# Column sums by GpSimd and fp32 matmuls in place of fp16 pairs, in a convolution fused with layer norms and a table-driven FFN

## What is computed

```python
def _ln_c(v): return (v - mean_c(v)) / sqrt(var_c(v) + 1e-6)       # over the 256 channels
x = x + conv3x3_mean(_ln_c(x))          # each channel by itself, all weights 1/9, zero border
t = tokens(x)                           # (8, 4096, 256)
n = (t - mean(t)) / sqrt(var(t) + 1e-5)
t = t + ffn(n)                          # ffn returns n plus the small additions below
```

## Time and profile before

| | |
|---|---|
| median of 3 runs | 748.62 us (745.1 to 753.97) |
| the profiled execution | 747.69 us, span 745.9 us |
| busy: PE, DVE, ACT, POOL | 546.9, 593.3, 496.0, 295.8 us |
| mean granted TensorE clock | 0.903 |
| DMA | 68.01 MB, mean 91 GB/s; DVE waits for a load once, 20.5 us, at the start |
| waits, in total: DVE L568 for PE | 62.6 us in 41 |
| waits, in total: PE L932 for DVE g | 67.8 us in 27 |

### The profile page before, as it was taken

The page is one execution under the profiler, slowest core; times in us unless marked ns, Lnnn a source line. Parts: engine busy times, 40 slices in busy tenths (PEclk is TensorE's granted clock), DMA queues, the critical chain, the costliest instruction groups (busy, mean ns, idle before and its releaser), DMA issues. The chain is left out here.

```text
span 745.9 us, 11144 instructions
## 1 busy us (share of the span) xinstructions
PE 546.9 (73%) x2381; PEld 268.0 (36%) x2423; DVE 593.3 (80%) x1482; ACT 496.0 (66%) x739; POOL 295.8 (40%) x580
## 2 busy tenths in 40 slices
PE   0045578888888888777889887768888888889670
PEld 0011234444434344333344343334434443444340
DVE  1679888998898888688798988968898888897240
ACT  0113677778787778747687867667788777788830
POOL 0223644544444444443244444414444444442200
PEclk9987899999999999969898989899999999999985
DMA  9999990993679544990469707940329009497999
GB/s 109 107 164 195 189 158 1 115 177 48 82 101 178 93 56 73 167 159 0 57 101 175 119 1 112 126 45 0 52 30 145 0 1 118 23 77 43 89 83 77
DMA packets 626041, 68.01 MB, mean 91 GB/s; under 512 B 625856, under 2 KB 625984, under 8 KB 625984
## 3 DMA queue, kind: packets, MB, share of 16 engines
q1 hardware_dynamic: 624496, 67.29, 79.8%
q10 hardware_dynamic: 1488, 0.17, 0.2%
HBM read 33.90 MB, written 33.55 MB: 90 GB/s over the span
## 5 line engine op out<-in xcount | busy, mean ns | idle before, releaser
L831 ACT ACTIVATE xbuf<-xbuf,shift,gain (+1 forms) x256 | 222.1, 935 | 0.0
L678 POOL TENSOR_TENSOR nlo<-n,nhi 128x1024 f16<-128x1024 f32 x64 | 152.4, 2382 | 124.0 <-ACT nhi L813 124.0
L550 DVE BATCH_NORM_STATS2 stat<-xbuf 128x6 f32 (+1 forms) x256 | 171.5, 683 | 20.6 <-DMA xbuf<-x 20.5
L910 PE MATMUL ps<-h1m,w2m 128*128 128x512 f32 x256 | 142.0, 638 | 0.0
L568 DVE TENSOR_TENSOR xbuf<-ps,xbuf 128x512 f32 (+1 forms) x128 | 90.8, 709 | 62.7 <-PE ps L871 62.6
L541 DVE TENSOR_SCALAR n<-xbuf,stat,rns 128x256 f32 (+1 forms) x256 | 133.1, 595 | 1.1
L813 ACT ACTIVATE nhi<-n 128x1024 f16<-128x1024 f32 x64 | 67.9, 1062 | 93.1 <-DVE n L541 93.1
L871 PE MATMUL ps<-nhi,band 128*128 128x512 f16 (+1 forms) x408 | 116.6, 402 | 16.1 <-POOL nlo L678 14.1
L871 PE MATMUL ps<-nlo,band 128*128 128x512 f16 (+1 forms) x408 | 119.6, 411 | 0.0
L800 ACT ACTIVATE h<-ps 128x512 f32<-128x512 f32 x128 | 76.4, 597 | 60.2 <-PE ps L913 59.7
L688 POOL TENSOR_TENSOR ut<-xbuf,stat 128x16 f32<-128x16 f32 x32 | 7.3, 227 | 252.7 <-DVE shift L469 252.7
(11 more groups left out here) (91 smaller groups left out, 651.2 us busy)
## 6 DMA issues: line engine op xcount, KB each, us to landing
xbuf<-x SPq DMA_DIRECT2D x16, 1024.0 KB, 11.6
out<-xbuf SPq DMA_DIRECT2D x32, 512.0 KB, 7.1
xbuf<-x SPq DMA_DIRECT2D x30, 512.0 KB, 7.0
out<-xbuf SPq DMA_DIRECT2D x12, 1024.0 KB, 12.8
out<-xbuf SPq DMA_DIRECT2D x16, 256.0 KB, 7.9
xbuf<-x SPq DMA_DIRECT2D x4, 256.0 KB, 8.2
consts<-cst SPq DMA_DIRECT2D x1, 170.0 KB, 2.4
h<-ws ACTq DMA_DIRECT2D x8, 10.0 KB
```

The source lines that it names most:

```text
L550: return v.bn_stats(stat[:, j % 4, at + 2 * s:at + 2 * s + 2, :].rearrange("p w n -> p (w n)"), xview(par)[:, w:w + 2, :].rearrange("p w c ...
L678: pool.tensor_tensor(nlo[:, at:at + HALF, :], n32[:, h, :, :], nhi[:, at:at + HALF, :], ALU.subtract).then_inc(lo_ready, 1)
L831: ins = act.activation(col, col, ACT.Identity, bias=shift[:, k, w:w + 1], scale=gain[:, k, w:w + 1])
L910: pe.matmul(ps[:, B_L2, :], w2m[:, :], h1m[:, i % 2, :], start=False, stop=False)
```

## The change

- n32 becomes a ring of 16 columns. POOL sums it over three neighbouring columns in fp32 into `nsum`: an edge sum of one column (it completes the last column of the chunk before), then three adds of up to four columns each. One fp32 matmul per bank by the band matrix replaces the six. ACT's nhi and POOL's nlo are gone.
- The FFN's remainder is one fp32 tensor h1r with one fp32 matmul; the biases ride in two of its unused rows. DVE's two h1lo per step and the bias matmul are gone.
- thr lies in SBUF; picks no longer wait for g.
- DVE's order: compare, rank, put(0), put(1), top come before the eight normalisations, the rest of the burst between the later additions and statistics ("flags, then burst"). POOL decodes first and sums after.
- Setup: two of four copies of the remainder's weights are loaded, and the bias tile, the band cast and some setup instructions go.

DVE, the stretch in the middle of a step, before: flags after the normalisations, the picks' result (ysel) after an addition.

The core of the diff (left out are setup, names of tensors and semaphores, and the guards of POOL's decoding):

```diff
--- before.py
+++ after.py
@@ -461,10 +440,7 @@
                 elif i == 3:
                     lnc.count(v.scalar_tensor_tensor(rstd[:, k, :], s_nu[:, :], 1.5, s_r0[:, :], ALU.add, ALU.mult))
                 elif i == 4:
-                    c = t - 7
-                    if not known(t) or c >= 0:
-                        v.wait_ge(yt_done, c + 1)
-                    v.tensor_scalar(rns[:, :], rstd[:, k, 0:CW], SCALE / 9.0, None, ALU.mult)
...
@@ -535,12 +511,13 @@
                         c, jc, par = norm
                         if w == 0:
                             v.wait_ge(fin_ready, t)
-                        if w % HALF == 0:
-                            wait(v, lo_ready, 2 * c + w // HALF - 1)
+                            wait(v, sum_ready, c - 1)
+                        if w == CW - 1:
+                            wait(v, sum_ready, c)
                         k = (j - 1) % 4
-                        ins = v.tensor_scalar(n32[:, w // HALF, w % HALF, :], xview(par)[:, jc * CW + w, :],
+                        ins = v.tensor_scalar(n32[:, (jc * CW + w) % RING, :], xview(par)[:, jc * CW + w, :],
                                               stat[:, k, w, 1:2], rns[:, w:w + 1], ALU.subtract, ALU.mult)
-                        if w % HALF == HALF - 1:
+                        if w in (1, CW - 1):
...
@@ -626,36 +592,35 @@
                 wait_x1(0)
                 finish(3)
                 x1_statistics(0)
-                x_statistics(1)
                 finish(4)
                 finish(5)
+                x_statistics(1)
+                compare()
+                x_statistics(2)
+                rank()
+                put(0)
+                put(1)
+                top()
                 for w in range(CW):
                     normalise(w)
-                compare()
                 add_convolution(1)
-                rank()
-                x_statistics(2)
+                put(2)
                 wait_x1(1)
-                top()
+                put(3)
                 x1_statistics(1)
-                low_parts(2)
                 add_convolution(2)
-                put(0)
                 counted = x_statistics(3)
-                put(1)
                 wait_x1(2)
-                put(2)
+                put(4)
                 x1_statistics(2)
-                put(3)
+                put(5)
                 add_convolution(3)
-                put(4)
                 wait_x1(3)
-                put(5)
+                put(6)
...
@@ -671,12 +636,39 @@
                 tok = chunk_at(t, j, pair, 3)
                 k4 = (j - 3) % 4
 
-                def low_parts(h):
+                def edge_sum():
+
                     c, jc, par = norm
-                    at = (jc * CW + h * HALF) % RING
-                    pool.wait_ge(hi_ready, 2 * c + h + 1)
-                    pool.tensor_tensor(nlo[:, at:at + HALF, :], n32[:, h, :, :], nhi[:, at:at + HALF, :],
-                                       ALU.subtract).then_inc(lo_ready, 1)
+                    a = jc * CW % RING
+                    pool.wait_ge(n_ready, 2 * c + 1)
+                    wait(pool, conv_done, 4 * c - 4)
+                    if jc == 0:
+                        ins = pool.tensor_tensor(nsum[:, 0, :], n32[:, 0, :], n32[:, 1, :], ALU.add)
+                    else:
+                        last = (a - 1) % RING
+                        ins = pool.tensor_tensor(nsum[:, last, :], nsum[:, last, :], n32[:, a, :], ALU.add)
+                    ins.then_inc(edge_ready, 1)
+
+                def column_sums():
+
+                    c, jc, par = norm
+                    a = jc * CW % RING
+                    b = a + CW
+                    pool.wait_ge(n_ready, 2 * c + 2)
+                    pool.tensor_tensor(nsum[:, a + 1:b:2, :], n32[:, a:b:2, :], n32[:, a + 1:b:2, :],
+                                       ALU.add).then_inc(sums, 1)
+                    pool.wait_ge(sums, 2 * c + 1)
+                    if a > 0:
+                        ins = pool.tensor_tensor(nsum[:, a:b:2, :], nsum[:, a + 1:b:2, :], n32[:, a - 1:b - 2:2, :],
+                                                 ALU.add)
+                    else:
+                        if jc > 0:
+                            pool.tensor_tensor(nsum[:, 0, :], nsum[:, 1, :], n32[:, RING - 1, :], ALU.add)
+                        ins = pool.tensor_tensor(nsum[:, 2:b:2, :], nsum[:, 3:b:2, :], n32[:, 1:b - 2:2, :], ALU.add)
+                    ins.then_inc(sums, 1)
+                    pool.wait_ge(sums, 2 * c + 2)
+                    pool.tensor_tensor(nsum[:, a + 1:b - 2:2, :], nsum[:, a + 1:b - 2:2, :], n32[:, a + 2:b:2, :],
+                                       ALU.add).then_inc(sum_ready, 1)
 
                 if tok:
...
@@ -744,6 +729,9 @@
                     ins.then_inc(feat_ready, 1)
                     dc.end()
                     pool.wait_ge(feat_ready, c + 1)
+                if norm:
+                    edge_sum()
+                    column_sums()
 
...
@@ -785,8 +773,8 @@
                         if tile[1] % 2 == 0:
                             act.wait_ge(l1r_done, 2 * tile[2] + tile[1] // 2 + 1)
                             wait(act, l2_done, tau - 2)
-                            act.activation(h1hi[:, tile[1] // 2, :], ps[:, B_L1R, :],
-                                           ACT.Relu).then_inc(h1hi_ready, 1)
+                            act.activation(h1r[:, tile[1] // 2, :], ps[:, B_L1R, :],
+                                           ACT.Relu).then_inc(h1r_ready, 1)
                         act.wait_ge(l1m_done, tau + 1)
                         wait(act, l2_done, tau - 1)
...
@@ -802,15 +790,9 @@
                     if s == 0 and ffn:
                         c, jc, par = ffn
                         act.wait_ge(ft_done, c + 1)
-                        wait(act, l2_done, 4 * c - 4)
+                        wait(act, l1m_done, 4 * c - 4)
                         act.activation(featT[:, jc % 2, :, :].rearrange("p a n -> p (a n)"), ftp,
                                        ACT.Copy).then_inc(ft_copied, 1)
-                    if norm and s < 2:
-                        c, jc, par = norm
-                        at = (jc * CW + s * HALF) % RING
-                        act.wait_ge(n_ready, 2 * c + s + 1)
-                        wait(act, conv_done, 2 * (2 * c + s) - 5)
-                        act.activation(nhi[:, at:at + HALF, :], n32[:, s, :, :], ACT.Copy).then_inc(hi_ready, 1)
                     if s == 3 and (not known(t) or t <= NCHUNK + 1):
...
@@ -852,25 +834,14 @@
             def convolve(conv, s):
 
                 c, jc, par = conv
...
-                        pieces += [(i, 1, (w + d + i) % RING) for i in range(2) if 0 <= w + d + i < W]
+                at = (jc * CW + 2 * s) % RING
                 wait(pe, x1_done, 4 * c + s - 1)
-                if s in (0, 1, 3):
-
-                    pe.wait_ge(lo_ready, 2 * c + (1 if s == 0 else 2 if s == 1 or jc == CHUNKS - 1 else 3))
-                n = 0
-                for src in (nhi, nlo):
-                    for i, k, at in pieces:
-                        n += 1
-                        ins = pe.matmul(bank[:, i:i + k, :], band[:, :], src[:, at:at + k, :],
-                                        start=n == 1, stop=n == 2 * len(pieces))
-                ins.then_inc(conv_done, 1)
+                if s == 0:
+                    pe.wait_ge(sum_ready, c + 1)
+                elif s == 3 and jc < CHUNKS - 1:
+                    pe.wait_ge(edge_ready, c + 2)
+                pe.matmul(ps[:, B_CONV + s % 2, :], cst[:, K_BAND:K_BAND + P], nsum[:, at:at + 2, :],
+                          start=True, stop=True).then_inc(conv_done, 1)
 
             def step(t, j, pair):
                 conv = chunk_at(t, j, pair, 2)
...
@@ -905,12 +876,9 @@
                         tau, i, c, jc = tile
                         pe.wait_ge(h1m_ready, tau + 1)
                         wait(pe, h2_ready, tau)
-                        pe.matmul(ps[:, B_L2, :], w1[:, T_BIAS, :], featT[:, jc % 2, i // 2, :], start=True,
-                                  stop=False)
-                        pe.matmul(ps[:, B_L2, :], w2m[:, :], h1m[:, i % 2, :], start=False, stop=False)
-                        pe.matmul(ps[:, B_L2, :], w2r[:, i % 2, :], h1hi[:, i // 2, :], start=False, stop=False)
-                        pe.wait_ge(h1lo_ready, 2 * c + i // 2 + 1)
-                        pe.matmul(ps[:, B_L2, :], w2r[:, i % 2, :], h1lo[:, i // 2, :], start=False,
+                        pe.matmul(ps[:, B_L2, :], w2m[:, :], h1m[:, i % 2, :], start=True, stop=False)
+                        pe.wait_ge(h1r_ready, 2 * c + i // 2 + 1)
+                        pe.matmul(ps[:, B_L2, :], w2r[:, i % 2, :], h1r[:, i // 2, :], start=False,
                                   stop=True).then_inc(l2_done, 1)
                     if s == 2 and back:
...
@@ -925,11 +893,9 @@
                         c = last[0]
```

(4 more changed lines are left out.)

127 lines of the change are left out of this document (44 added, 83 removed).

## The result

The changed kernel takes 842.12 us (median of 5 runs, 839.36 to 846.36), the kernel before 750.68 on the same chip (5 runs, 745.1 to 758.3). The ratio is 1.124, 95% interval 1.118 to 1.130; it is taken over the undisturbed runs alone, and so it isn't quite the quotient of the two medians. The forecast was 832, with a range of 765 to 890.

A forecast was written before the change was run, and what follows sets the result against it. DVE was taken as the bound. A full step was 19.15 + 1.7 + 1.25 + 0.6 + 0.6 = 23.3 us against 20.2; 27 steps at 3.1 added 84 us to 748.6, giving 832 us, range 765 to 890.

The forecast's parts named there:

- the later sums: POOL's second and third long adds would hold up DVE's ym, hot and one-hot add: 1.25 us per step.
- if the second add gets in before ym: Upper side for the later sums: POOL's second add starts before DVE's ym, costing 2.2 us more per step.
- Removed from DVE: Two h1lo (1.2 us) and gw's hold-up (0.72 us) go per step; DVE's own work falls from 18.45 to 16.5 us.
- First cost: DVE asks for PE's picks (ysel) too early and waits 2.65 us with everything queued behind; step 19.15 us.
- Second cost: DVE's flags stand beside POOL's sums: 1.7 us at ycar, then 1.25 us at ym, hot and the one-hot add.
- wrong if ycar is short (A): Sign in the changed trace: ycar takes about 1.8 us instead of 0.2; a short ycar would point to A.
- Third: POOL's decoding runs beside DVE's eight normalisations and lengthens them: 0.6 us per step, bounds 0 and 1.9.
- Fourth: PE idles longer and its clock falls to the lower level: 0.6 us per step, bounds 0 and 2.
- D: Rival: picks arrive in time, the 2.65 us wait goes, the other terms stay: 769 us; within B's 12%.
- A: Rival: POOL's fp32 adds and DVE's flags don't block each other; step 19.5 us, 730 us; 8%.
- B: Rival: only ycar stands, clock no worse than in the best step; step 20.85 us, 766 us; 12%.
- C: Rival: PE at its lower level in the sums' chain; step 26 us, 906 us; 8%.

The follow-up runs named there:

- x6: Kernel before with only the FFN part: remainder as one fp32 tensor with one fp32 matmul, h1lo gone, bias matmul kept; 751.0 us beside 748.9.
- x2: Changed kernel with put(0) and put(1) (ysel, yy) moved behind the normalisations and the second bank's addition; 781.63 us, ratio 1.043 to before.
- x4: Changed kernel with ACT's eight wide activations dealt 0, 4, 4, 0 instead of 0, 3, 3, 2; 807.83 us, ratio 1.078 to before.
- x3: Changed kernel with the edits of x1 and x2 together; 745.5 us, ratio 0.989 to before.
- x5: Changed kernel with each of POOL's long adds issued as two shorter ones, same sums and places; 833.75 us beside 748.9 of before.
- x7: x3 with the epsilons, s_var's second input, in PSUM too; 741.94 us, 0.991 of before.
- x1: Changed kernel with yy, yc, ym, ycar and hot in PSUM instead of SBUF; 803.32 us, ratio 1.067 to before.
- x8: x7 with the last of POOL's sums issued in two parts, the first part releasing bank 0 early; 700.87 us beside 748.9 of before.
- x9: Control: kernel before with yy, yc, ym, ycar, hot and the epsilons in PSUM, nothing else changed; 754.08 us, ratio 1.002 to before.

## Why the prediction was right, and where it was off

For the step 628.15 to 651.35 the terms can be measured one by one, against the forecast's base of 16.5 us of DVE's own work. The step bears this base out: DVE is busy 20.27 us of it, 16.06 without what the table lists as stands, and 0.48 are small gaps. One step can be a lucky one, so the last column has the mean of the 27 full steps, t = 6 to 32, in us per step:

| term | predicted | measured in this step | mean of 27 steps |
|---|---|---|---|
| ysel waits for the picks | 2.65 | 2.17 | 2.79 |
| the first long sum catches one instruction | 1.7 (ycar) | 2.01 (ym, 2.19 - 0.18) | 2.40 (ym, yc, ycar) |
| the later sums | 1.25 | 0.65 (hot, 1.08 - 0.43) + 0.99 (L486, 1.39 - 0.40) | 1.37 (hot, L486) |
| normalisations beside decoding | 0.6 | 0.56 (4.50, was 3.94) | 0.36 |
| clock | 0.6 | not separable | not separable |
| reciprocal waits for the square root | 0 | 0.28 | 0.49 |
| step | 23.3 | 16.5 + 6.66 = 23.16; the window shows 23.20 | 16.5 + 7.41 = 23.91; the trace shows 24.12 |

The stands in the last column are what these instructions lasted above the shortest of their kind in the run, the normalisations what they lasted above that less the same in before. The step that was read comes so close to the forecast because its deviations cancel: -0.48, +0.31, +0.39, -0.04, and 0.28 for the reciprocal in place of 0.6 for the clock. In the mean the stands are the term that was sized too small: 3.77 against 2.95. In some steps the case occurs that the forecast gave as its upper side, "if the second add gets in before ym": at 138.22 yc stands 2.32 us beside the first sum and ym, right behind it, as long beside the second.

*What bounded the kernel.* DVE, as the earlier trace rows had it, but with PE close behind, which the text ahead weighed too lightly (x6). For this forecast it made little difference, because both new costs fall on DVE itself. One row was named wrongly: L908 at 558.33 is the second layer's bias matmul, and the first layer of the new chunk (L900) goes just ahead of it, at 558.11. The sum isn't changed by that.

*Removed from DVE.* gw is at 343 ns in the mean, the two h1lo are gone, as expected. That DVE's saving would become waiting was the right sentence. In x6 it does so even in the old order, there with PE's second layer longer too.

*First cost, the early read.* Right in kind and place: ysel waits in all 32 steps. The last five, where the pipeline empties, make 30.4 us of it (longest 10.9); the 27 before them 75.3, a mean of 2.8 against the 2.65 of the forecast. x2 removes the 75.3, x4 shortens them to 31.4 through ACT alone. The 30.4 of the end aren't owed to the early read: x2 and x3, which read late, have 27.2 and 28.7 there. The forecast had what is queued behind ysel, too: top, eight normalisations, the sums.

*Second cost.* The mechanism was right, and its first place one instruction off. I let the first long sum begin 0.15 us after the last normalisation. It began 0.70 us after it, as the edge sum (0.73 us, at 641.13) went in only after the normalisations: decoding, which I had end beside them, was itself slowed (feat 1.43 for two against 1.23 in the earlier trace rows; hit 0.88). ycar and yc slipped through and ym was caught, at a like price. By the sign named ahead, "wrong if ycar is short (A)", this step would have counted against the forecast; ym's 2.19 us, and ycar's 1711 ns in the mean of x2, where ysel and yy stand ahead of it, show that the sign named the instruction too narrowly and the mechanism holds. The adds came out at 2.35 us per 1024 and 1.8 to 1.9 per 768, where I took 2.14 and 1.65 from nlo with a fixed part of 0.1 that no row shows; with the 1.27 of x5 for 512 and 0.73 for 256 they lie on 0.19 us + 2.12 ns per element. The Trainium skill (GPSIMD Engine Reference, "Elementwise — side-by-side cycle accounting"), cited ahead with an estimate of 7.3 us for the four adds, was nearer: 0.73 + 2.35 + 2.36 + 1.86 = 7.3 us in the steps with four adds and 7.5 in this step's form, which has five instructions, against 6.6 of my sum.

*Which instructions stand.* With one of the two inputs moved to PSUM, s_var goes from 1102 to 175 ns (x7); ym, whose output moved along with an input, goes from 1756 to 183 (x1). With POOL's instructions halved, ym's time goes to 974 (x5). The Trainium skill's rule (SBUF — State Buffer, "SBUF: two separate sides") is that whichever of a DVE instruction with two SBUF inputs or in a two-port mode and a GpSimd instruction (for two SBUF inputs, one that reads SBUF) starts first keeps the shared ports for its whole length, and the other is fully blocked; these runs agree with it. g, newly of that kind with thr in SBUF, took 678 ns in the mean and 692 at most: never caught, as I had left it.

*Third, normalisations beside decoding:* 0.56 against 0.6 in the step that was read, all of it in the two normalisations beside feat (0.86 and 0.83 us, the other six 0.56 to 0.59). Over the run the mean is 637 ns, where before has 596 and x2 602, so per step it is 0.36 and the term was taken too high; what exactly made the difference I didn't test.

*Fourth, the clock:* granted 0.87 over the run, 0.903 before. PE's matmuls at the lower level (1.86 us for a bank at 641.91, 1.08 at 629.19) come right after its waits for the sums, but DVE waits for banks only 13.8 us in the whole run, so 0.4 us per step is the most it can have cost there. No run shows the 0.6 of the forecast. What the sum put at nothing, though the text and rival D have 0.3 for it, is the reciprocal's wait for the square root.

*The rivals.* A (no blocking) falls with ym, hot and L486. B (one stand only) falls with hot and L486, D (the picks are in time) with ysel's 105.7 us. C (PE at its lower level decides) falls with the 13.8 us. But once both costs are mended, the sums' chain that A and C speak of is exactly what is left: x3 and x7 are held by it, at 20.3 to 20.5 us per step, and x8 opens it.

*The whole:* 27 steps at 3.1 made 84 us. In the traces the 27 steps run from reciprocal to reciprocal, 114.81 to 672.93 us in before and 119.71 to 770.91 in the changed kernel: 93.1 us more, or 24.12 - 20.67 = 3.45 per step. The twenty steps of the ledger have 2.9; the first three (28.4 us for the very first, 18.9 in before) and the last four of the 27 make up the rest, at 5.0 each. The base of 20.2 was below before's 20.67 because its windows leave out the longest steps of before. Ahead of the 27 the changed kernel loses another 4.9 us, behind them 0.6. The emptying of the pipeline adds nothing:

```profile
L454 DVE RECIPROCAL s_r<-s_sqrt x34: 241/244/255, 27.3 to 688.2; 128x16 f32<-128x16 f32 x34
L433 DVE RECIPROCAL s_r<-s_sqrt x34: 252/253/254, 27.2 to 787.6; 128x16 f32<-128x16 f32 x34
```

From the last reciprocal to the end of the span it is 745.9 - 688.2 = 57.7 us in before and 844.5 - 787.6 = 56.9 now; ysel's longer waits there stand where before waits for ysel and for h1lo. Together 93.1 + 4.9 + 0.6 is 98.6, by which the spans differ. The medians differ by 91.4, since the profiled execution was the slowest of the changed kernel's five. That 832 came within 10 us owes something to luck: the stands were sized 0.8 us per step too small, and a base 0.5 too low, with the 0.6 of the clock that no run shows, made up for most of it.

## What to carry to other kernels

Before a read is moved earlier in an in-order queue, add up when its producer's own queue delivers, and count everything that is behind the read: here 0.22 us of work held up a step by 2 to 3 us. When long POOL instructions with SBUF inputs are added, list the DVE instructions with two SBUF inputs that can meet them; one input in PSUM took the stand away from them, at no cost that the control x9 could show, where shorter POOL instructions only halved ym's. And when an engine's relief brings nothing (x6, x7), look for the chain that is next and let its first consumer go early: with both costs mended, issuing one sum in two parts was worth 41 us, where the two savings of DVE's work (x6, x7) were worth none.

## What the runs showed of the hardware

- A stand moves. Taken from ym and hot (x1), 31.7 us of it reappeared at s_var, several instructions later; only when s_var was mended too (x7) was it gone, apart from yy, whose two inputs are still in SBUF and which takes some 0.6 us in x8.
- It works both ways: POOL's small instructions grew beside back-to-back normalisations (hit, 24 elements, 0.88 us), and those in turn by 14% (4.50 against 3.94 us for eight) in the step read here, by 7% in the mean of the run (637 against 596 ns).
- In the changed kernel and in the mended ones alike, the lower clock of PE follows its waits for the sums; with one bank released early the granted clock was 0.924 instead of 0.904, with no change to the matmuls.
- An extra POOL instruction of the same sum cost 0.22 us (x5), and its fp32 adds 2.12 ns per element and lane.
- Not tried: how far the kernel before would go with an early release of its own, and whether x8's remaining 28.6 us for the picks can be had, all of it in the last five steps, where the pipeline empties.
